# Turned exponentials in blocks of 512 columns, new instruction orders, and cosines on GpSimd, in an attention and feed-forward kernel

## The reference, cut to what matters

```python
q = apply_rope((x @ Wq) heads, pos)            # 32 heads of 64, halves rotated by cos and sin
k = apply_rope((x @ Wk) heads, pos)            # 8 heads, each used by 4 query heads
scores = einsum('bhqd,bhkd->bhqk', q, k) / sqrt(64), causal mask
attn = softmax(scores); out = einsum('bhqk,bhkd->bhqd', attn, v)
x = x + out @ Wo
x = x + ffn(layernorm(x))                      # per-token int8 quantisation, int8 weight, float16 result
```

## Time and profile before

| what | value |
|---|---|
| runs | 999.88, 1001.14, 1000.58 us, median 1000.58 |
| profiled execution | 999.45 us, span 997.6 us |
| busy: TensorE matmul, VectorE, ScalarE, GpSimd | 851.1, 787.2, 672.4, 567.5 us |
| ScalarE high copies (L668), 512 | 224.0 us |
| VectorE low copies (L844), 512 | 247.0 us |
| VectorE maxima (L851), 512 | 247.2 us |
| VectorE cosine products (L813), 96 | 110.1 us, mean 1147 ns |
| ScalarE exponential of 128 keys, and the read of its sum | 363 ns, 203 ns |
| ScalarE kept high part of a rotated tile | 629 ns |
| GpSimd weight split (L323, L327), 32 of each | 47.0 and 58.0 us |
| GpSimd issue of a value load (L297), 64 | mean 757 ns; waits for attends 87.1 us in 29 waits |
| placed queries, issue to landing | 2.3 us |
| ScalarE waiting for turns (L668) | 154.3 us in 317 waits |

### The profile page before, as it was taken

One profiled execution on the slowest core, in us unless ns is written; L12 is line 12 of the kernel. 1 busy time (PEld: TensorE's weight loads), 2 busy tenths in 40 slices (PEclk: granted clock), 3 DMA queues, 4 the chain that ended last, 5 costly groups with the idle time before them and its releaser, 6 DMA issues.

```text
span 997.6 us, 24967 instructions
## 1 busy us (share of the span) xinstructions
PE 851.1 (85%) x8488; PEld 695.4 (70%) x8488; DVE 787.2 (79%) x1869; ACT 672.4 (67%) x1954; POOL 567.5 (57%) x492
## 2 busy tenths in 40 slices
PE   2978999998999989998999998889999998998632
PEld 1757777777777777777777777777777777777511
DVE  5778888787877787887778777888787777778797
ACT  1557777776777777777767776777777776777533
POOL 3146665555566666655565666666556665564026
PEclk9999999999999999999999999999999999999955
DMA  7134434343344334343333343343434343432002
GB/s 234 43 80 93 95 80 92 79 93 79 86 96 91 88 86 91 84 94 77 89 83 88 94 93 83 86 95 82 90 82 90 82 94 89 92 75 64 1 17 69
DMA packets 52396, 84.80 MB, mean 85 GB/s; under 512 B 12592, under 2 KB 19504, under 8 KB 52272
## 3 DMA queue, kind: packets, MB, share of 16 engines
q1 hardware_dynamic: 46640, 66.43, 28.6%
q0 software_dynamic: 5632, 16.78, 6.8%
HBM read 18.15 MB, written 2.10 MB: 20 GB/s over the span
## 4 chain that ended last, share of the span: by engine, by line
PE 39%; DVE 28%; issue 11%; DMA 7%; ACT 5%; POOL 5%; SPq 4%; ACTq 0%; POOLq 0%; DVEq 0%
PE x_bank L405 18%; DVE raw L813 6%; PE t_bank L485 6%; DVE probT L844 5%; DVE neg_max L851 5%; PE o_bank L498 5%; PE s_bank L471 4%; DMA qT<-wv 4%; PE s_bank L472 3%; DMA swp<-raw 3%; DVE oT L873 2%; DVE o_norm L865 2%; SPq L239 2%; ACT oT L676 2%; DVE resid L883 2%
## 5 line engine op out<-in xcount | busy, mean ns | idle before, releaser
L668 ACT ACTIVATE probT<-t_bank 128x384 f16<-128x384 f32 (+3 forms) x512 | 224.0, 438 | 156.9 <-PE t_bank L485 154.3
L851 DVE TENSOR_REDUCE neg_max<-s_bank 128x1 f32<-128x384 f32 (+3 forms) x512 | 247.2, 483 | 38.5 <-PE s_bank L473 38.2
L659 ACT ACTIVATE prob<-s_bank,neg_max 128x384 f32<-128x384 f32 (+3 forms) x512 | 267.7, 523 | 0.2
L485 PE MATMUL t_bank<-ident,prob 128*128 128x128 f32 x1280 | 230.5, 278 | 40.8 <-DVE probT L844 34.7
L844 DVE SCALAR_TENSOR_TENSOR probT<-t_bank,probT 128x384 f16<-128x384 f32 (+3 forms) x512 | 247.0, 482 | 12.0 <-ACT probT L668 8.7
L337 POOL TENSOR_TENSOR swp<-swp,sin 128x512 f32<-128x512 f32 x96 | 128.2, 1336 | 182.1 <-DMA swp<-raw 181.9
L498 PE MATMUL o_bank<-vg,probT 128*128 128x64 f16 x3840 | 196.5, 193 | 20.7 <-DVE o_norm L865 19.9
L471 PE MATMUL s_bank<-kT,qT 128*128 128x384 f32 (+3 forms) x512 | 195.0, 381 | 6.4 <-DMA qT<-wv 6.2
L498 PEld LDWEIGHTS o_bank<-vg,probT 128*128 128x128 f16 x3840 | 167.6, 98 | 43.6 <-issue 33.8
L485 PEld LDWEIGHTS t_bank<-ident,prob 128*128 128x128 f32 x1280 | 138.1, 141 | 54.0 <-ACT prob L659 37.6
L405 PE MATMUL x_bank<-xT,wg 128*128 128x512 f32 x576 | 159.2, 412 | 13.0 <-DVE resid L883 12.9
(11 more groups left out here) (87 smaller groups left out, 1033.3 us busy)
## 6 DMA issues: line engine op xcount, KB each, us to landing
qT<-wv SPq DMA_DIRECT2D x248, 128.0 KB, 2.3
swp<-raw SPq DMA_DIRECT2D x384, 64.0 KB, 2.0
wg_raw<-in_w_group POOLq DMA_DIRECT2D x32, 384.0 KB, 3.6
vg<-value POOLq DMA_DIRECT2D x64, 64.0 KB, 2.4
resid<-in_x SPq DMA_DIRECT2D x4, 512.0 KB, 10.3
out<-resid SPq DMA_DIRECT2D x16, 128.0 KB, 1.7
prob<-in_w_out SPq DMA_DIRECT2D x6, 256.0 KB, 7.7
qT<-qT SPq DMA_DIRECT2D x8, 128.0 KB, 2.3
```

Of the source, the lines that this page charges most:

```text
L485: last = nc.tensor.transpose(unit_bank(u)[:, k * P:(k + 1) * P], prob[u % 4][:, k * P:(k + 1) * P], ident[:, :])
L659: nc.scalar.activation(prob[u % 4][:, 0:n], s_bank[slot % 4][:, 0:n], ACT.Exp, bias=neg_max[:, slot % 4:slot % 4 + 1], accum_out=row_sum[: ...
L668: nc.scalar.activation(probT[u % 4][:, HI, 0:n], unit_bank(u)[:, 0:n], ACT.Copy, scale=PROB_SCALE).then_inc(probT_hi, 1)
L851: nc.vector.tensor_reduce(neg_max[:, slot:slot + 1], s_bank[slot][:, 0:n], AX.X, ALU.max, negate=True).then_inc(max_done, 1)
```

## The change

All loops are written out for the 32 steps, and the step is cut differently:

- Score groups. The 16 units become 11 groups: all four heads of the first quarter (128 keys) in one bank, one unit per bank for 512 and 384 keys, two heads per bank for 256 keys. `maxima` is one instruction per group. There are three `s_bank`s; the fourth bank is `ot_bank`, used for turned outputs alone.
- Blocks. A block is 128 keys of all four heads, 512 columns, and a step has ten. The exponentials are written to a ring of five such blocks (`prob`, 5 x 4 x 128), so a unit of 512 keys writes four pieces of 128 columns. `turn` turns one block (four heads), `keep_probT` and `keep_probT_low` handle 512 columns, `attend` multiplies one block for four heads, reading `value` directly. `vg` and `load_values` are gone.
- The cosine products of steps 1 to 31 move from VectorE to GpSimd; those of step 0 stay on VectorE.
- Each engine has a new order within the step, written out call by call; tiles 0 and 1 of a step are projected one step earlier than before (tile 0 in the middle, tile 1 near the end of the step before the last one), tile 2 early in the step before.

In the diff, cut to its core, the calls of each order stand several to a line.

```diff
-LAG = 3
-ATTEND_LAG = 2
-PROJECT_AT = {1: 0, 2: 1, 5: 2}
-ROTATE_AT = {4: 0, 6: 1, 8: 2}
-HIGH_AT = {6: 0, 8: 1, 10: 2}
+SCORE_GROUPS = ((0, (0, 1, 2, 3)), (1, (0,)), (1, (1,)), (1, (2,)), (1, (3,)),
+                (2, (0,)), (2, (1,)), (2, (2,)), (2, (3,)), (3, (0, 1)), (3, (2, 3)))
+BLOCKS = tuple((v, k) for v in range(Q_TILES) for k in range(QUERY_TILES[v] + 1))
+FIRST_BLOCK = tuple(BLOCKS.index((v, 0)) for v in range(Q_TILES))
+SCORE_BANKS, TURN_BANKS, PROBS, TURNED = 3, 2, 5, 4
...
             def turn(s, t):
+                pe.wait_ge(exp_done, unit_no(s, BLOCKS[t][0], GROUP_HEADS))
+                if B >= TURN_BANKS:
+                    pe.wait_ge(probT_lo, B - TURN_BANKS + 1)
+                for h in range(GROUP_HEADS):
+                    last = nc.tensor.transpose(t_bank[B % TURN_BANKS][:, h * P:(h + 1) * P], prob[:, B % PROBS, h, :], ident[:, :])
...
+                act.wait_ge(max_done, G + 1)
+                if first_block + blocks > PROBS:
+                    act.wait_ge(turned, first_block + blocks - PROBS)
+                nc.scalar.activation(prob[:, slot:slot + blocks, h, :],
+                                     s_bank[G % SCORE_BANKS][:, at * n:(at + 1) * n].rearrange("p (k n) -> p k n", n=P),
+                                     ACT.Exp, bias=neg_max[:, s % 2, u:u + 1], ...)
...
+            # SP, each step
+                swap_halves(s + 1, 2); place_queries(s + 1, 0); swap_halves(s + 2, 0)
+                place_queries(s + 1, 1); swap_halves(s + 2, 1)
+            # GpSimd, each step
+                keep_low(s + 1, 0)
+                rotate_first(s + 1, 1); rotate_second(s + 1, 1); rotate_sum(s + 1, 1)
+                rotate_first(s + 1, KEYS); rotate_second(s + 1, KEYS); rotate_sum(s + 1, KEYS)
+                keep_low(s + 1, 1); keep_low(s + 1, KEYS)
+                split_group_weights(s + 3); load_group_weights(s + 5)
+                rotate_second(s + 2, 0); rotate_first(s + 2, 0); rotate_sum(s + 2, 0)
+            # TensorE, before the first step
+            project(1, 0); project(1, 1); scores(0, 0 to 3)
+            # TensorE, each step
+                turn(s, 0); scores(s, 4); scores(s, 5); project(s + 1, 2); turn_output(s - 1, 3)
+                scores(s, 6); turn(s, 1); attend(s, 0); turn(s, 2); out_product(s - 1, 3)
+                scores(s, 7); turn(s, 3); scores(s, 8); scores(s, 9); turn_output(s, 0)
+                turn(s, 4); project(s + 2, 0); scores(s, 10); turn(s, 5)
+                attend(s, 1); attend(s, 2); attend(s, 3); attend(s, 4)
+                turn(s, 6); out_product(s, 0); turn_output(s, 1); turn(s, 7)
+                attend(s, 5); attend(s, 6); turn(s, 8); out_product(s, 1); attend(s, 7)
+                turn(s, 9); project(s + 2, 1); turn_output(s, 2); scores(s + 1, 0)
+                attend(s, 8); attend(s, 9); scores(s + 1, 1); scores(s + 1, 2)
+                out_product(s, 2); scores(s + 1, 3)
+            # ScalarE, each step (e = exponentials, p = keep_probT)
+                e(s, 1, 0); e(s, 1, 1); p(s, 0); e(s, 1, 2); keep_high(s + 1, 0); e(s, 1, 3)
+                keep_oT(s - 1, 3); keep_raw(s + 1, 2); p(s, 1); p(s, 2)
+                e(s, 2, 0); e(s, 2, 1); e(s, 2, 2); p(s, 3); p(s, 4); e(s, 2, 3)
+                keep_raw(s + 2, 0); keep_oT(s, 0); e(s, 3, 0); e(s, 3, 1); keep_high(s + 1, 1)
+                p(s, 5); p(s, 6); e(s, 3, 2); keep_oT(s, 1); e(s, 3, 3); p(s, 7)
+                keep_high(s + 1, KEYS); p(s, 8); p(s, 9); keep_oT(s, 2); keep_raw(s + 2, 1)
+                e(s + 1, 0, 0 to 3)
+            # VectorE, each step (m = maxima, l = keep_probT_low, n = normalise_output, i = invert_sums)
+                n(s - 1, 3); m(s, 3); m(s, 4); m(s, 5); l(s, 0); keep_oT_low(s - 1, 3); m(s, 6)
+                i(s, 0); l(s, 1); add_product(s - 1, 3); n(s, 0); l(s, 2); m(s, 7); m(s, 8)
+                l(s, 3); m(s, 9); l(s, 4); m(s, 10); keep_oT_low(s, 0); i(s, 1); n(s, 1)
+                l(s, 5); l(s, 6); add_product(s, 0); keep_oT_low(s, 1); l(s, 7); add_product(s, 1)
+                i(s, 2); l(s, 8); n(s, 2); l(s, 9); m(s + 1, 0); keep_oT_low(s, 2); i(s, 3)
+                m(s + 1, 1); m(s + 1, 2); add_product(s, 2)
```

More of the change, by code:

```diff
@@ L171, in attention_ffn_kernel, with tile_no, group_no, block_no @@
         block = ctx.enter_context(nc.Block())
[L172 to L210, removed]
+        def tile_no(s, j):
+            return s * PROJ_TILES + j
+        def group_no(s, a):
+            return s * len(SCORE_GROUPS) + a
+        def block_no(s, t):
+            return s * len(BLOCKS) + t
+        def unit_no(s, v, h):
+            return s * UNITS + v * GROUP_HEADS + h
+        def part_no(s, v):
+            return s * Q_TILES + v
+        def units_through(G):
+            s, a = G // len(SCORE_GROUPS), G % len(SCORE_GROUPS)
+            v, heads = SCORE_GROUPS[a]
+            return unit_no(s, v, heads[-1]) + 1
+        def inside(s):
+            return 0 <= s < STEPS
         @block.sync
@@ L370, in _, with keep_low @@
-            all_steps(pool, step)
+                nc.gpsimd.tensor_tensor(raw[j][:, :], raw[j][:, :], swp[j][:, :], ALU.add).then_inc(rope_done, 1)
+            def keep_low(s, j):
+                if not inside(s):
+                    return
+                T = tile_no(s, j)
+                pool.wait_ge(hi_kept, T + 1)
+                high, low = (kT[s % 2][:, HI, :], kT[s % 2][:, LO, :]) if j == KEYS else query_parts(s, j)
+                nc.gpsimd.tensor_tensor(low, raw[j][:, :], high.bitcast(f32), ALU.subtract).then_inc(lo_kept, 1)
@@ L450, in _ @@
                         pe.wait_ge(pow_kept, 1)
[L451 to L453 removed]
+                    project(0, j)
             pe.wait_ge(fw_cast, 1)
@@ new lines, in attend @@
+            def attend(s, t):
+                if not inside(s):
+                    return
+                B, b, g = block_no(s, t), s // KV_HEADS, s % KV_HEADS
+                v, k = BLOCKS[t]
+                pe.wait_ge(probT_lo, B + 1)
+                if k == 0 and part_no(s, v):
+                    pe.wait_ge(o_normed, part_no(s, v))
+                for h in range(GROUP_HEADS):
+                    for a, c in ((HI, HI), (HI, LO), (LO, HI)):
+                        last = nc.tensor.matmul(o_bank[:, h * HEAD_DIM:(h + 1) * HEAD_DIM], probT[B % TURNED][:, a, h, :],
+                                                value[:, c, b * Q_TILES + k, g * HEAD_DIM:(g + 1) * HEAD_DIM],
+                                                start=(k == 0 and h == 0 and (a, c) == (HI, HI)),
+                                                stop=(k == QUERY_TILES[v] and (a, c) == (LO, HI)), skip_group_check=True)
+                last.then_inc(pv_done, 1)
@@ L558, in _ @@
[L558 to L565 removed]
+            pe.wait_ge(v_lo, TOK_TILES)
+            pe.wait_ge(fwT_kept, 1)
+            project(1, 0)
+            project(1, 1)
@@ L861, in normalise_output @@
+            def normalise_output(s, v):
+                if not inside(s):
+                    return
+                J = part_no(s, v)
                 dve.wait_ge(inv_done, J + 1)
-                if not (isinstance(J, int) and J == 0):
+                if J:
                     dve.wait_ge(o_turned, J)
```

700 lines of the change are left out of this document (389 added, 311 removed).

## The result

The changed kernel takes 881.89 us in the median of 4 runs (880.41 to 882.80), against 1000.23 us before; the ratio is 0.882, with a 95% interval from 0.8798 to 0.8842. The forecast was 920 us with a range down to 893: the direction was right, the gain was larger than the range allowed. The profiled execution took 882.80 us for a span of 881.0.

What follows compares the result with a forecast made beforehand. TensorE's work plus stalls from late VectorE and ScalarE work was taken as the bound. 154.1 + 31 x 24.6 = 916.7 us of span, 919.7 with the offsets to the median, said as 920; range 893 to 960.

Steps and rivals of the forecast that it cites:

- TensorE's work, 23.9 us: TensorE in each step: matmuls, turns and weight loads keep their shapes in another order, so 23.9 us stay.
- The stalls: TensorE's waits per step after the change: the walk gave 24.3 to 24.4 us, taken as 24.6, over 23.9 of work.
- rival B: Steps: no stall and cheaper weight loads from adjacent score groups, 23.5 us per step, 886 us; chance 0.13.
- The start: Before the first turn: two early projects of step 1 move it from 69.20 to about 74.4 us, +5.2 us.
- The end: After the steps' stretch: last step 2.75 us shorter, but the last output chain stands alone before the statistics, +1.9 us.
- the walk through the orders: One step followed through all engines' orders with the trace's durations: 24.3 to 24.4 us per step.
- the hold ahead of block 7: TensorE before block 7 in each step: held about 0.2 us by the low half of block 5.
- the one ahead of block 8: TensorE before block 8 in each step: held 0.25 us by the last exponential of quarter 3.
- the strided exponentials: ScalarE writing 128-column pieces 2 KB apart: taken at no cost, upper bound over 6 us per step.
- the narrow places: Four places in the step with 0 to 0.4 us to spare, among them next step's first scores awaiting placed queries.
- the part which pays: VectorE in each step: three cosine products gone, 3.4 us, its work falling from 21.7 to about 17 us.
- Rival C: GpSimd's ring with ScalarE becomes the bound: no faster from 1.80 us per operation, 1075 us at 2.0; chance 0.05.

Runs made afterwards that it cites:

- the experiment with the first scores: Changed kernel with the first scores ahead of the two early projects, and the first exponentials ahead of these projects' copies: 883.17 us, ratio 0.8834.

## Why the prediction was wrong

**The step that failed is TensorE's work, 23.9 us, taken as the floor of the step and as unchanged by the order.** The span came out 35.7 us below the forecast, in three terms.

- The step: 23.39 instead of 24.6, 31 x 1.21 = 37.5 us. Of the 1.21, 0.82 is the count: I took the price of each kind from one place and used it everywhere. Four turns cost 0.45 ahead of attends, as in my row, but 0.36 to 0.39 ahead of scores, projects and out products; a score unit of 512 keys costs 0.52 to 0.62 in the old order where I took 0.63, one of 384 keys 0.42 to 0.50 for my 0.50. The turns were 0.36 too dear in sum and the score units 0.30, the projects 0.11 and the attends 0.07. 0.48 is the new order's own saving, which I priced at nothing with a bound of 0.4: score units 0.34 and turns 0.17 less, turned outputs 0.06 more. In the new order score units stand next to each other, which they never did in the old one, and 12 of the 40 turns stand ahead of attends instead of 30; the attends, in longer runs too, gain nothing (3.53 and 3.51). The stalls were nearly right: 0.7 taken, 23.39 - 22.60 = 0.79 measured, and 0.82 + 0.48 - 0.09 = 1.21. Both errors of the work went the same way, and rival B, made for this side, had its floor at 23.5 since it subtracted only 0.4 from the same wrong count; so the range ended at 893.
- The start: the first turn at 79.93, not 74.4, 5.5 us late. The projects start at 67.77, 1.3 later than I let them; from there to the first scores at 74.13 it is 6.4 us, where I had 3.9, at a granted clock of about 0.52 (rows at the end); the rest lies in the scores, still at the lower level, and in the maxima and exponentials. By the experiment with the first scores this term is not even on the path: step 0 ends with GpSimd.
- The end: 80.54 became 75.87, and I had 79.7. The last step shrank by 4.46 us (917.06 to 942.26 before, 805.13 to 825.87 after), 0.5 more than the mean step did, and why is open: neither kernel has a project in its last step. From the last output's sum but one to the last statistics 9.64 became 9.76, where I added 1.9: VectorE's wait for the root fell from 2.71 to 0.28 us, since ScalarE loads the table for it (1.28 us) at 827.56, before the root is asked for, and not at 945.42, inside that wait, as before.

**What held.** That TensorE's stalls could go and nearly did: 4.3 us per step before (27.35 - 23.08; I had 3.4), 0.8 after. That the walk through the orders found the hold ahead of block 7 (0.2 by the walk, 0.19 measured); the one ahead of block 8 (0.25) did not come. That the strided exponentials, the grouped maxima and the 512-column copies cost what the nearest rows showed. That GpSimd runs at its short duration when VectorE has no second SBUF input. That the placed queries were among the narrow places: they are the largest wait that is left, in 12 steps out of 32, where I had 0.4 us to spare.

**What I attributed wrongly.** I called the cosine product the part which pays. Of the 3.97 us per step (by the key tile's copy), with the cosines on VectorE in both kernels the rest of the change (orders, blocks, groups, banks) brings 27.38 - 25.37 = 2.01, 0.48 of it as cheaper work of TensorE; moving the cosines brings the other 1.96. And that move pays only together with the rest: alone it costs 0.94 per step. Rival C, GpSimd's ring, was real, but I had it hang on the duration of its operations. In both runs in which it came the operations took 1.28 us, and all three tiles were projected in the step just before their use.

**What stays open.** How the 2.01 divides between the order, the score groups, the separate bank for turned outputs and the direct reading of the values was not separated. Only the size of the copies was, at most 0.1 us, and the direct reading changes nothing in TensorE's own work. Why the placed queries come late in some steps and in time in others was not asked, nor what removes the short waits ahead of blocks 1 and 7.

## What to carry to other kernels

Before forecasting a kernel whose fullest engine also waits, measure that engine's work with all else left out: a price read at one place of a running trace is not the price at the others, and many small errors of one sign add up. An operation moved off a busy queue pays only if its new place is not in series with the next stage; look for the longest ring through the transfers and count everything that stands in it. Where two engines can hold each other up, the price of an operation is that of its collisions, and a new schedule changes it: the same product took 1365 ns in the median in one order and 1640 in the other.

## What the runs showed of the hardware that I had not expected

The 258 matmuls of a step, in the same shapes, take 23.08 us in one order and 22.60 in another with nothing to wait for. The two projects at the start took 2.90 and 2.93 us for six matmuls (1.64 in the steps, both from the first start to the last end). The windows view of the changed kernel around them (columns as in the earlier trace rows) shows the granted clock, the last number but two, at 0.52, near the lower of its two levels of 1.2 and 2.4 GHz, behind a stretch in which TensorE's matmuls were busy 7.08 of 11 us:

```profile
55.00:66.00 11.00, 7.08 (x28) 4.75 (x28) 9.74 (x16) 5.82 (x12) 7.38 (x5) 1.00 0.38 84
66.00:80.00 14.00, 11.92 (x38) 8.28 (x39) 2.38 (x4) 5.83 (x15) 4.14 (x5) 0.52 0.27 67
80.00:100.00 20.00, 19.73 (x234) 17.24 (x232) 14.41 (x29) 15.48 (x41) 14.96 (x12) 1.00 0.35 80
```

A float32 product of VectorE with two SBUF inputs took 677 ns at best and up to 2429 beside GpSimd. In a collision the one that came second paid. In the kernel before VectorE's product started first ten times, by some 0.05 us, and took 692 ns each time, while GpSimd's took 1.77 to 1.79 us (the one in the earlier trace rows is such a case); where GpSimd's started first it kept its 1.27 to 1.30 us and VectorE's ended some 0.55 us after it.
